# Layer norm by a centering product, with squares on ScalarE, in a kernel of eight chained layers

## What is computed

```python
def _layernorm(x, axis=-1, eps=1e-05):
    m = jnp.mean(x, axis=axis, keepdims=True)
    v = jnp.var(x, axis=axis, keepdims=True)
    return (x - m) / jnp.sqrt(v + eps)
x = _layernorm(x + _L0_attn_ref(x, ...), axis=-1)
x = _layernorm(x + _L0_ffn_ref(x, ...), axis=-1)
...
x = _layernorm(x + _L3_ffn_ref(x, ...), axis=-1)
```

## Time and profile before

| | us |
|---|---|
| median of 3 runs (2516.85 to 2520.87) | 2520.08 |
| span of the profiled execution (no other time is shown for it) | 2518.8 |
| TensorE, VectorE, ScalarE, GpSimd busy | 2042.3, 1821.2, 1370.8, 254.7 |
| statistics (line 104, 336 times), aggregation (line 110, 336 times) | 70.1, 26.8 |
| normalising on VectorE (line 123, 168 times), on ScalarE (line 155, 168 times) | 56.5, 63.3 |

### The profile page before, as it was taken

How to read it: one execution, slowest core, us unless ns; L and a number is a source line. 1 busy time by engine, 2 the same in 40 slices (tenths; PEclk the granted TensorE clock), 3 DMA queues, 4 the chain that set the end, 5 groups by cost and what they waited for, 6 DMA issues and landing times. The chain is left out here.

```text
span 2518.8 us, 50950 instructions
## 1 busy us (share of the span) xinstructions
PE 2042.3 (81%) x17646; PEld 1272.0 (51%) x17653; DVE 1821.2 (72%) x4153; ACT 1370.8 (54%) x3474; POOL 254.7 (10%) x321
## 2 busy tenths in 40 slices
PE   6988986956849999667499999998576867774987
PEld 5787774425534444345344444444443554453675
DVE  2232235878968999768688888888788778777776
ACT  4344444743535555464477777776455545553554
POOL 1000001200012122100122222221000000000000
PEclk6555557977959999889799999999777877776786
DMA  1000000000000000000000000000000000000000
GB/s 46 3 3 4 3 3 25 17 35 1 0 28 19 25 22 22 13 1 1 24 22 23 21 23 21 21 23 6 15 13 12 0 12 12 12 0 27 2 1 17
DMA packets 26957, 36.56 MB, mean 15 GB/s; under 512 B 4042, under 2 KB 24138, under 8 KB 26564
## 3 DMA queue, kind: packets, MB, share of 16 engines
q1 hardware_dynamic: 26820, 34.59, 4.4%
HBM read 33.53 MB, written 1.05 MB: 14 GB/s over the span
## 5 line engine op out<-in xcount | busy, mean ns | idle before, releaser
L795 ACT ACTIVATE m_h<-ps 128x512 f32<-128x512 f32 x520 | 310.5, 597 | 277.8 <-PE ps L746 277.6
L815 DVE TENSOR_TENSOR m_hwlo<-m_hw,m_hwhi 128x512 f16<-128x512 f32 x523 | 366.0, 700 | 0.3
L833 DVE TENSOR_TENSOR m_hw<-m_h,ps 128x512 f32<-128x512 f32 x388 | 266.8, 688 | 89.5 <-ACT m_h L795 77.9
L788 ACT ACTIVATE m_hwhi<-m_hw 128x512 f16<-128x512 f32 x523 | 325.4, 622 | 1.5 <-DVE m_hw L833 1.5
L426 DVE TENSOR_TENSOR rn_s_lo<-rn_s_full,rn_s_hi 128x32 f16<-128x32 f32 x512 | 98.5, 192 | 240.2 <-ACT rn_s_full L406 234.4
L746 PE MATMUL ps<-x_hi,m_whi 128*128 128x512 f16 x652 | 247.7, 380 | 4.7 <-issue 4.4
L746 PE MATMUL ps<-x_lo,m_whi 128*128 128x512 f16 x652 | 247.9, 380 | 0.0
L746 PE MATMUL ps<-x_hi,m_wlo 128*128 128x512 f16 x652 | 247.9, 380 | 0.0
L404 ACT ACTIVATE rn_s_hi<-ps 128x32 f16<-128x32 f32 x512 | 101.3, 198 | 205.0 <-PE ps L383 173.7
L752 PE MATMUL ps<-m_hwhi,m_whi 128*128 128x512 f16 x529 | 201.1, 380 | 1.7 <-DVE m_hwlo L815 1.7
L752 PE MATMUL ps<-m_hwhi,m_wlo 128*128 128x512 f16 x529 | 200.1, 378 | 0.0
(11 more groups left out here) (442 smaller groups left out, 4750.5 us busy)
## 6 DMA issues: line engine op xcount, KB each, us to landing
m_stage<-in_m_w SPq DMA_DIRECT2D x97, 128.0 KB, 2.0
m_stage<-in_m_w SPq DMA_DIRECT2D x33, 192.0 KB, 2.3
lj_w<-in_lj_w SPq DMA_DIRECT2D x6, 768.0 KB, 4.3
lq_w<-in_lq_w SPq DMA_DIRECT2D x1, 1536.0 KB, 6.0
m_sel<-in_c_sel_pairs SPq DMA_DIRECT2D x2, 661.5 KB
la_w<-in_la_w SPq DMA_DIRECT2D x1, 1280.0 KB, 5.4
out<-ln_x SPq DMA_DIRECT2D x4, 256.0 KB, 2.7
rn_a<-in_L_attn_a SPq DMA_DIRECT2D x1, 512.0 KB, 3.4
```

Source lines behind the costliest of these rows:

```text
L788: nc.scalar.activation(hw_hi[:, k % 4, :], hw[:, k % 2, :], ACT.Copy).then_inc(hi_done, 1)
L795: nc.scalar.activation(h[:, k % 2, :], ps[:, 4 + (3 * k % 4 if gated else k % 2), :], func)\
L815: nc.vector.tensor_tensor(hw_lo[:, k % 4, :], hw[:, k % 2, :], hw_hi[:, k % 4, :], ALU.subtract)\
L833: nc.vector.tensor_tensor(hw[:, k % 2, :], src[:, k % 2, :], cb, ALU.mult).then_inc(hw_done, 1)
```

## The change

The transposes at the start become products with the centering matrix (identity minus 1/128 everywhere), so that each block arrives in PSUM turned and with its mean taken off. The matrix is one more input and one more DMA, ahead of the tokens' on SP's queue. ScalarE squares each block of 128 rows and sums the squares along it (`accum_out`), into the tile ln_ms; the squares themselves go to ln_x and are overwritten. The root takes the sum with a scale of 1/128. Normalising is then one multiplication with the reciprocal: on VectorE for groups 0, 2 and 3, on ScalarE (a Copy with a scale) for group 1. The way back is unchanged.

```diff
             for g in range(G):
                 for j in range(4):
                     i = 4 * g + j
-                    last = nc.tensor.transpose(ps[:, g, j * C:(j + 1) * C], src[:, i * P:(i + 1) * P], ident[:])
+                    last = nc.tensor.matmul(ps[:, g, j * C:(j + 1) * C], src[:, i * P:(i + 1) * P], S.center[:],
+                                            start=True, stop=True)
                 last.then_inc(rows_in, 1)
...
             def normalise(g):
                 for i in range(4 * g, 4 * g + 4):
-                    last = nc.vector.tensor_scalar(rows[:, i, :], ps[:, g, i % 4 * C:(i % 4 + 1) * C], mv[:, i, 0:1],
-                                                   rstd[:, i:i + 1], ALU.subtract, ALU.mult)
+                    last = nc.vector.tensor_scalar(rows[:, i, :], ps[:, g, i % 4 * C:(i % 4 + 1) * C],
+                                                   rstd[:, i:i + 1], None, ALU.mult)
                 last.then_inc(normed_dve, 1)
 
-            statistics(0)
-            aggregate(0)
-            statistics(1)
             scales(0)
-            aggregate(1)
             normalise(0)
             scales(1)
             normalise(2)
+            normalise(3)
...
         @block.scalar
         def _(act):
-            for h in range(2):
+            def squares(g):
+                act.wait_ge(rows_in, g + 1)
+                for i in range(4 * g, 4 * g + 4):
+                    last = nc.scalar.activation(rows[:, i, :], ps[:, g, i % 4 * C:(i % 4 + 1) * C], ACT.Square,
+                                                accum_out=ms[:, i:i + 1])
+                return last
+
+            def deviations(h):
                 half = slice(h * HT, (h + 1) * HT)
-                act.wait_ge(aggr_s, h + 1)
-                nc.scalar.activation(std[:, half], mv[:, half, 1], ACT.Sqrt, bias=S.eps_ap(eps)).then_inc(std_s, 1)
-                g = 2 * h + 1
-                act.wait_ge(shift_s, h + 1)
-                for i in range(4 * g, 4 * g + 4):
-                    last = nc.scalar.activation(rows[:, i, :], ps[:, g, i % 4 * C:(i % 4 + 1) * C], ACT.Identity,
-                                                bias=shifts[:, i:i + 1], scale=rstd[:, i:i + 1])
-                last.then_inc(normed_act, 1)
+                act.wait_ge(sq_s, h + 1)
+                nc.scalar.activation(std[:, half], ms[:, half], ACT.Sqrt, bias=S.eps_ap(eps), scale=1.0 / C)\
+                    .then_inc(std_s, 1)
+
+            squares(0)
+            squares(1).then_inc(sq_s, 1)
+            squares(2)
+            deviations(0)
+            squares(3).then_inc(sq_s, 1)
+            act.wait_ge(rstd_s, 1)
+            for i in range(4, 8):
+                last = nc.scalar.activation(rows[:, i, :], ps[:, 1, i % 4 * C:(i % 4 + 1) * C], ACT.Copy,
+                                            scale=rstd[:, i:i + 1])
+            last.then_inc(normed_act, 1)
+            deviations(1)
...
             sp.dma_start(S.ident[:], A["c_ident"]).then_inc(got, 16)
             sp.dma_start(S.identb[:], A["c_identb"]).then_inc(got, 16)
+            sp.dma_start(S.center[:], A["c_center"]).then_inc(got, 16)
             sp.dma_start(rows[:], A["L0_attn_tokens"].rearrange("b t c -> (b t) c")
```

More of the change, by code:

```diff
@@ L63, in layernorm_phase @@
 def layernorm_phase(nc, S, src, dst, eps=LN_EPS, gain=None, shift=None, out=None, sync=None, pool=None):
-    rows_in, stats_s, aggr_s, std_s, rstd_s, shift_s, normed_dve, normed_act, back, stored, turned, high_s = S.sems.new(
-        "ln_rows_in", "ln_stats", "ln_aggr", "ln_std", "ln_rstd", "ln_shift", "ln_normed_dve", "ln_normed_act",
-        "ln_back", "ln_stored", "ln_turned", "ln_high")
+    rows_in, sq_s, std_s, rstd_s, normed_dve, normed_act, back, stored, turned, high_s = S.sems.new(
+        "ln_rows_in", "ln_squares", "ln_std", "ln_rstd", "ln_normed_dve", "ln_normed_act", "ln_back", "ln_stored",
+        "ln_turned", "ln_high")
     G = NT // 4
@@ L71, in layernorm_phase @@
     ps, ident = S.psum, S.ident
-    with (nc.sbuf_tensor(f"ln_stat{S.sems.n}", [P, NT, 6], F32) as stats,
-          nc.sbuf_tensor(f"ln_mv{S.sems.n}", [P, NT, 2], F32) as mv,
+    with (nc.sbuf_tensor(f"ln_ms{S.sems.n}", [P, NT], F32) as ms,
           nc.sbuf_tensor(f"ln_sd{S.sems.n}", [P, NT], F32) as std,
           nc.sbuf_tensor(f"ln_rs{S.sems.n}", [P, NT], F32) as rstd,
-          nc.sbuf_tensor(f"ln_nm{S.sems.n}", [P, NT], F32) as shifts,
           nc.sbuf_tensor(f"ln_x{S.sems.n}", [P, NT, C], F32) as rows,
@@ L80, in wait_normed @@
         def wait_normed(engine, g):
-            engine.wait_ge(normed_act if g % 2 else normed_dve, g // 2 + 1)
+            if g == 1:
+                engine.wait_ge(normed_act, 1)
+            else:
+                engine.wait_ge(normed_dve, g + 1 - (g > 1))
         @block.tensor
@@ L99, in _ @@
         def _(dve):
[L100 to L111, removed]
             def scales(h):
-                half, theirs = slice(h * HT, (h + 1) * HT), slice(h * HT + 4, (h + 1) * HT)
+                half = slice(h * HT, (h + 1) * HT)
                 dve.wait_ge(std_s, h + 1)
@@ L117, in scales @@
                 dve.wait_ge(rstd_s, h + 1)
-                nc.vector.scalar_tensor_tensor(out=shifts[:, theirs], in0=mv[:, theirs, 0], scalar=-1.0,
-                                               in1=rstd[:, theirs], op0=ALU.mult, op1=ALU.mult).then_inc(shift_s, 1)
             def normalise(g):
                 for i in range(4 * g, 4 * g + 4):
-                    last = nc.vector.tensor_scalar(rows[:, i, :], ps[:, g, i % 4 * C:(i % 4 + 1) * C], mv[:, i, 0:1],
-                                                   rstd[:, i:i + 1], ALU.subtract, ALU.mult)
+                    last = nc.vector.tensor_scalar(rows[:, i, :], ps[:, g, i % 4 * C:(i % 4 + 1) * C],
+                                                   rstd[:, i:i + 1], None, ALU.mult)
                 last.then_inc(normed_dve, 1)
-            statistics(0)
-            aggregate(0)
-            statistics(1)
             scales(0)
-            aggregate(1)
             normalise(0)
@@ L204, in _ @@
         def _(pe):
-            pe.wait_ge(got, 48)
+            pe.wait_ge(got, 64)
             for g in range(4):
@@ L2073, in build @@
           nc.sbuf_tensor("identb", [P, P], BF16) as identb,
+          nc.sbuf_tensor("center", [P, P], F32) as center,
           nc.sbuf_tensor("epsilons", [P, 3], F32) as epsilons):
         S.psum, S.xT, S.rT, S.ident, S.identb, S.epsilons = ps, xT, rT, ident, identb, epsilons
-        S.x_hi, S.x_lo = x_hi, x_lo
+        S.x_hi, S.x_lo, S.center = x_hi, x_lo, center
         S.eps_ap = lambda e: epsilons[:, S.eps.index(e):S.eps.index(e) + 1]
@@ L2095, in layout @@
     L["c_identb"] = np.eye(P, dtype=bf16)
+    L["c_center"] = np.eye(P, dtype=f) - f(1.0 / C)
     L["L0_attn_tokens"] = I["L0_attn_tokens"]
```

## The result

| | before | after |
|---|---|---|
| median of 4 runs each, us | 2520.47 (2516.85 to 2525.3) | 2532.65 (2530.61 to 2534.23) |
| span of the profiled execution, us | 2518.8 | 2530.4 (2532.13 for that execution) |
| ratio of the runs | | 1.0053, 95% interval 1.0038 to 1.0069 |

The change makes the kernel slower by half a per cent, about 12 us where 22 were forecast.

The account below looks back on a forecast made before the run. Each layer norm was taken as a single file: first group up, chain to the last normalised row, tail of 3.99 us. Changes by kind of layer norm, plus 0.4 for the DMA, summed to +22.3: time 2542.4 us, range 2531 to 2560.

Parts of the forecast that it names:

- the load on the path: ScalarE's table load, moved from the block's start to behind twelve squares: 1.54 us on the path, 12 times.
- the product's two records: TensorE's centering product: two records per block, 0.238 us instead of 0.119; the price is only that groups come later.
- ScalarE's chain: ScalarE's squares, table load, roots and four copies, which the path to the last normalised row must pass through.
- drain rival: ScalarE drains before each table load: twelve loads cost 7 to 15 us more, 2550 to 2558; 7 in 100.
- root to end: From a layer norm's first root to its end: squares, copies, second root, reciprocal, eight multiplications and tail, 9.07 us.
- the tail: VectorE's split into halves at the layer norm's end, 3.99 us, taken over from the kernel before.
- The clock of the slow blocks: Layer norms at half clock throughout: fourth group at 7.0, end 15.9 us; +0.2 against 15.69, +2.3 against 13.63.
- Between the blocks: Phases between the layer norms: forecast change 0.
- The clock falling under the products: Rival: eleven full-clock layer norms lose the clock like 530.4, each ending 1.5 us later: +16, 2559; 8 in 100.
- The faster rival: Longer products raise the clock of phases behind layer norms: 25 us at the most, 2517; 4 in 100.

Follow-up runs that it names:

- the early load: Changed kernel plus a one-column root at the head of ScalarE's part, so the table load stands there again: 2509.99 us, 0.9966 of the kernel before.
- the transposes: Changed kernel with transposes back in place of the centering products, the mean not taken off: 2510.53 us in one execution.
- the product alone: Kernel before with only the centering product in place of the transposes; statistics, shifts and normalisation split stay: 2537.89 us in one execution.
- the early root: Changed kernel with the table load at the head and ScalarE's second root before its four copies: 2502.92 us, 0.9932 of the kernel before.

## Why the prediction was right, and where its size was off

**The direction** rested on the load on the path, the product's two records and ScalarE's chain. All three stand. The load: the experiment that moves it takes 14.5 us out of the blocks; forecast were 12 x 1.54 = 18.5. Blocks with and without it differ by 14.39-12.98 = 1.41, 12 times 16.9, and the dummy root hands back 0.19 of each by delaying the first square. The drain rival is refuted by the row: the twelfth square starts at 1824.32, the next slot would be at 1824.57, the load starts at 1824.77 and the root 0.01 after its end. Here the Trainium skill (ScalarE: Activation LUTs, What ACT_TABLE_LOAD costs) agrees on the 1283 ns, and its 1380 ns of drain is not seen: 0.2.

**The step that was mis-sized: "root to end", 9.07.** It measures 14.39 - 5.67 = 8.72. In the timeline after, the root and four squares take 1.2 as forecast, but the copies go at 0.25 each and not 0.30, 0.2 less for the four, and the tail is 3.82, not 3.99, because the first two casts now find both evacuations done (0.75 for the pair against 0.91 in the earlier trace rows). I had carried the tail over from before though it held a wait there. At 0.27 to 0.36 over 20 blocks that is 6.8 us, two thirds of the error of 10.7. The Trainium skill (ScalarE: Activation LUTs, What ACT_TABLE_LOAD costs) puts a pointer operand at about 93 ns; from 0.35, the start-to-start of the two-pointer Identity (1.51 for four, the last one 0.457 long), that gives an estimate of 0.26, nearer than my 0.30.

**The clock of the slow blocks** is part of the rest. I let a half-clock block stay at 0.50 for all its products. Under the longer work it rises before the end: the 32 records at 2289.9 take 5.96 us at a mean of 0.61, not 7. And the clock at the start is not the block's own: of the five later first layer norms of the loop one ran all its products at full clock (13.01) and four in part low (14.5), against 14.9 forecast for all; 1055.0 fell low where its kin before did not and lost 2.64 instead of 1.3. Rows of TensorE alone in the profile after:

```profile
533.40:537.60 4.20, 4.20 (x25) 0.61 0.00 0
...
1862.61:1866.45 3.84, 3.84 (x32) 1.00 0.64 205
2289.94:2295.90 5.96, 5.96 (x32) 0.61 0.01 3
```

**Between the blocks** I forecast nothing, and 2.6 us went. That is a sum of larger pieces: the last layer's phase takes 182.5 instead of 185.4 (-2.9) and two others 1.0 less each, while the first linear attention takes 1.8 more (27.7 for 26.0) and another phase 1.5. The last layer's phase took 182.2 to 183.7 in the profiles of all nine experiments, three of them with the old layer norm, so the profile before looks like the odd one, not the change. One piece does belong to the change and was not in the forecast: behind the last normalised row 3.67 us became 2.79, and the early load and the transposes show 2.79 too, the product alone 3.68. The medians, which do not depend on that one execution, differ by 12.2. The range holds the time by 1.7 us, less than the largest of these pieces and less than the spread of the executions: that it holds is in part luck.

**The rivals.** The clock falling under the products happened in one block (1055.0), and was worth 1.4 us there, not 16 in all. The faster rival did not come true for the change, but its mechanism is real: the phases behind a layer norm do wait for the clock, and "at the most 25 us" is near the 17 to 20 that ten idle transposes bring. What I had wrong is what raises it: with the longer work at the head alone the first 4 us behind the loop's layer norms stay at 0.50 to 0.56; work in the tail right before the barrier brings most of them to 1.00.

**Left open.** Why, in the changed kernel, the clock at the start of the loop's blocks differs from pass to pass (3.84 or 5.46 us for the same 32 records) was not settled, nor why linear attention left the low clock earlier with the early load alone.

## What to carry to other kernels
A table load is free only while it stands in front of nothing: a change that puts another function first moves the load onto the path, and a one-column dummy of the coming function brings it back. Before cutting the work of a busy engine, follow the chain of the small stage itself: here 96 us less of VectorE's work bought nothing until ScalarE's order was changed with it. And where phases are separated by barriers, look at the clock of the first microseconds behind each: here cheap dead work of TensorE in the tail was worth as much as the best reordering, 17 us each, though together with the reordering it made some of the layer norms themselves longer.

## What the runs showed of the hardware
- ScalarE squares with a running sum at 0.25 us per 128x128 block out of PSUM, accumulator read included; a Copy with a scale pointer goes at the same 0.25.
- A true f32 product of 128x128 by 128 is two TensorE records, 3.81 us for 32, against 1.94 for the 16 records of transposes.
- A VectorE operation of four numbers with two SBUF inputs lasted until GpSimd's running instruction ended, 1.07 us in the kernel before and 3.00 with the product alone, against 0.16 with GpSimd idle; operations with one input did not wait (0.58 for four either way).
- Four operations on one number each cost 0.58 us against 0.16 for one on four numbers: each full block grew by 0.83 from two such places.
- Ten dead transposes ahead of a barrier raised the granted clock of the first 4 us behind it from 0.50 to 1.00 in 11 of the loop's 12 phases with the early root, and in 5 of 12 in the kernel before.
